# The experts' second product of a mixture-of-experts stage, from rounded pieces instead of full-precision matmuls

## What is computed

```python
buf = zeros((E * cap + 1, Dx)).at[safe].set(x_rep)          # E = 8, cap = 4560, Dx = 192
z = 2.0 * buf
z = z * rsqrt(mean(z * z, axis=-1) + EPS) * norm_w[:, None, :]
gu = einsum('ecd,ehd->ech', z, w13)                          # first product, 192 -> 1024
g, u = split(gu, 2, axis=-1)
y = buf + einsum('ech,edh->ecd', silu(g) * u, w2)            # second product, 512 -> 192
y_tok = y.reshape(E * cap, Dx)[didx]
out = (cw[:, None] * y_tok).reshape(N, TOP_K, Dx).sum(axis=1)
```

## Time and profile before

| | |
|---|---|
| median of 3 runs | 3388.71 us |
| lowest and highest | 3383.93 and 3389.58 us |
| span of the profiled execution | 3385.4 us |
| TensorE busy in the span | 3004.5 us |
| VectorE, GpSimd, ScalarE busy | 2468.5, 2034.5, 1363.1 us |
| mean granted TensorE clock | 0.944 of full speed |

### The profile page before, as it was taken

How to read it: one execution, slowest core, us unless ns; L and a number is a source line. 1 busy time by engine, 2 the same in 40 slices (tenths; PEclk the granted TensorE clock), 3 DMA queues, 4 the chain that set the end, 5 groups by cost and what they waited for, 6 DMA issues and landing times.

```text
span 3385.4 us, 62750 instructions
## 1 busy us (share of the span) xinstructions
PE 3004.5 (89%) x20432; PEld 2601.3 (77%) x20432; DVE 2468.5 (73%) x6258; ACT 1363.1 (40%) x3398; POOL 2034.5 (60%) x1558
## 2 busy tenths in 40 slices
PE   2988889888889888898898898599999999999997
PEld 1777767777777777777777777598989898898987
DVE  3899998999998999989989987354444444444553
ACT  0434444344344344343443444343344443443443
POOL 2666666666666666666666664255555555555655
PEclk9899998999998999989988989799999999999999
DMA  6544544433333333233233320233333333433333
GB/s 190 150 131 138 155 126 138 130 85 102 90 89 103 82 97 103 77 101 99 80 101 89 90 75 23 68 51 62 52 67 49 66 57 56 69 50 65 51 62 48
DMA packets 205961, 297.49 MB, mean 88 GB/s; under 512 B 88374, under 2 KB 167675, under 8 KB 205874
## 3 DMA queue, kind: packets, MB, share of 16 engines
q1 hardware_dynamic: 82994, 243.82, 26.1%
q0 software_dynamic: 122880, 52.55, 11.1%
HBM read 201.73 MB, written 93.90 MB: 87 GB/s over the span
## 4 chain that ended last, share of the span: by engine, by line
issue 31%; POOL 27%; DVE 20%; DMA 12%; PE 7%; POOLq 1%; SPq 1%; ACT 1%; DVEq 0%; ACTq 0%
DMA out<-arena,who 10%; POOL out L1437 8%; POOL moe_rows L1268 6%; POOL qk L721 4%; POOL arena L689 4%; DVE hot L631 3%; DVE place L669 3%; POOL rstd L707 3%; POOL spread L697 3%; DVE arena L1419 2%; DVE pooled L498 2%; DVE pieces L550 2%; PE bank L1409 2%; DVE rot_s L535 1%; DMA prob<-in_w_t 1%
## 5 line engine op out<-in xcount | busy, mean ns | idle before, releaser
L1437 POOL DMA_INDIRECT out<-arena,who x320 | 597.2, 1866 | 202.9 <-issue 198.7
L721 POOL TENSOR_TENSOR qk<-rot_c,rot_s 114x768 f32<-114x768 f32 x256 | 455.2, 1801 | 256.7 <-DVE rot_s L535 253.6
L1395 ACT ACTIVATE arena<-bank 128x456 f32<-128x456 f32 x320 | 175.5, 549 | 634.2 <-PE bank L1386 621.8
L1409 PE MATMUL bank<-prob,arena 128*114 128x192 f32 x2560 | 429.3, 326 | 0.0
L689 POOL TENSOR_TENSOR arena<-arena 112x896 f32<-112x896 f32 x192 | 396.8, 2096 | 44.3 <-DMA arena<-in_x 44.3
L1409 PEld LDWEIGHTS bank<-prob,arena 128*114 128x114 f32 x2560 | 412.2, 178 | 0.0
L1268 POOL DMA_INDIRECT moe_rows<-row,slot x256 | 293.1, 1145 | 185.3 <-issue 185.3
L1401 DVE TENSOR_TENSOR arena<-bank,arena 128x456 f32<-128x456 f32 x320 | 201.7, 630 | 268.5 <-ACT arena L1395 256.6
L571 DVE TENSOR_REDUCE top<-bank 114x2 f32<-114x456 f32 (+1 forms) x576 | 332.0, 622 | 2.5 <-PE bank L903 2.0
L843 PE MATMUL bank<-w_qkv,xn_t 97*114 97x384 f32 x512 | 221.3, 561 | 109.4 <-DVE place L669 108.7
L1426 POOL TENSOR_TENSOR rms<-rms,minus_half 114x4 f32<-114x4 f32 x82 | 85.4, 1042 | 348.0 <-DVE rms L1324 348.0
(11 more groups left out here) (167 smaller groups left out, 7523.2 us busy)
## 6 DMA issues: line engine op xcount, KB each, us to landing
arena<-in_x SPq DMA_DIRECT2D x64, 2352.0 KB, 11.3
arena<-moe_rows SPq DMA_DIRECT2D x82, 363.4 KB
moe_rows<-filler SPq DMA_DIRECT2D x20, 1453.5 KB
out<-h SPq DMA_DIRECT2D x64, 171.0 KB
out<-arena,who POOLq DMA_INDIRECT x320
arena<-in_w_t SPq DMA_DIRECT2D x9, 512.0 KB
arena<-in_w_t SPq DMA_DIRECT2D x18, 256.0 KB
moe_rows<-row,slot POOLq DMA_INDIRECT x256
```

The costliest lines, as they stand in the source:

```text
L721: nc.gpsimd.tensor_tensor(dst, a, b, ALU.add).then_inc(qk_rotated[t], 1)
L1409: ins = nc.tensor.matmul(bank[6 + s // 2][0:TT, D * (s % 2):D * (s % 2 + 1)], hid[:, j, TT * s:TT * (s + 1)], w_dn[e_par][:, j, :], start= ...
L1437: nc.gpsimd.indirect_dma_start(out=out[:, :], out_offset=bass.IndirectOffsetOnAxis(ap=who[par][:, s:s + 1], axis=0), in_=ys[par][:, s, :], ...
```

## The change

`hid` and `w_dn` are each split into a rounded part (fp32r) and the rest. `expert_down` multiplies the rounded part of `hid` by both parts of `w_dn` side by side (384 columns), and the rest of `hid` by the rounded part of `w_dn` (192 columns). Each of the four row groups gets a bank of its own: 6 and 7 as before, and 0 and 1, which `expert_up` uses for j = 0 and 2. The row groups are done in two pairs: pair 1 (banks 0 and 1) first, pair 0 (banks 6 and 7) behind it, partly interleaved. Each bank then holds two sums of 192 columns, and `weigh_rows` adds both, in eight operations in place of four, with a wait of VectorE for itself between the first part and the second. `expert_up` of the next tile waits for `y_first`, which pair 1 of `weigh_rows` sets. ScalarE gets four more copies for each tile (`high_hid`), VectorE four more subtractions (`low_hid`); both get one more operation for each expert. The order of the two engines' programs is changed around them.

```diff
         def round_expert(act, e, par):
...
+            nc.scalar.activation(w_dn2[par][:, :, 0, :], w_dn[par][:, :, :], ACT.Copy).then_inc(w_rounded, 1)
         def split_expert(dve, e, par):
...
+            nc.vector.tensor_tensor(w_dn2[par][:, :, 1, :], w_dn[par][:, :, :], w_dn2[par][:, :, 0, :].bitcast(fp32),
+                                    ALU.subtract).then_inc(w_split, 1)
         def expert_up(pe, n, e_par, j):
...
+            if j == 0:
+                wait(pe, y_first, n)
+        def high_hid(act, n, j):
+            act.wait_ge(hid_made, 4 * n + j + 1)
             if j == 0:
-                wait(dve, down, n)
+                wait(act, down, n)
+            nc.scalar.activation(hid2[:, j, 0, :], hid[:, j, :], ACT.Copy).then_inc(hid_high, 1)
+        def low_hid(dve, n, j):
+            dve.wait_ge(hid_high, 4 * n + j + 1)
+            nc.vector.tensor_tensor(hid2[:, j, 1, :], hid[:, j, :], hid2[:, j, 0, :].bitcast(fp32),
+                                    ALU.subtract).then_inc(hid_low, 1)
+        DOWN = (6, 7, 0, 1)
         def expert_down(pe, n, e_par):
-            wait(pe, y_weighted, n)
-            for j in range(4):
-                pe.wait_ge(hid_made[j], n + 1)
-                for s in range(SUB):
-                    ins = nc.tensor.matmul(bank[6 + s // 2][0:TT, D * (s % 2):D * (s % 2 + 1)], hid[:, j, TT * s:TT * (s + 1)],
-                                           w_dn[e_par][:, j, :], start=(j == 0 and s % 2 == 0), stop=(j == 3),
-                                           skip_group_check=True)
-            ins.then_inc(down, 1)
+            for pair, j in ((1, 0), (1, 1), (1, 2), (0, 0), (1, 3), (0, 1), (0, 2), (0, 3)):
+                if pair == 1:
+                    pe.wait_ge(hid_low, 4 * n + j + 1)
+                    if j == 0:
+                        pe.wait_ge(hid_made, 4 * n + 3)
+                elif j == 0:
+                    wait(pe, y_weighted, n)
+                for s in (2 * pair, 2 * pair + 1):
+                    at = slice(TT * s, TT * (s + 1))
+                    nc.tensor.matmul(bank[DOWN[s]][0:TT, 0:2 * D], hid2[:, j, 0, at],
+                                     w_dn2[e_par][:, j, :, :].rearrange("p c n -> p (c n)"),
+                                     start=(j == 0), stop=False)
+                    ins = nc.tensor.matmul(bank[DOWN[s]][0:TT, 0:D], hid2[:, j, 1, at], w_dn2[e_par][:, j, 0, :],
+                                           start=False, stop=(j == 3))
+                if j == 3:
+                    ins.then_inc(down_first if pair else down, 1)
+        def weigh_rows(dve, n, par, pair):
+            if pair:
+                dve.wait_ge(down_first, n + 1)
+                dve.wait_ge(x_weighted, n + 1)
+            else:
+                dve.wait_ge(down, n + 1)
+            for part in range(2):
+                for s in (2 * pair, 2 * pair + 1):
+                    ins = nc.vector.scalar_tensor_tensor(
+                        out=ys[par][:, s, :], in0=bank[DOWN[s]][0:TT, D * part:D * (part + 1)], scalar=w_slot[par][:, s:s + 1],
+                        in1=ys[par][:, s, :] if part else xw[:, s, :], op0=ALU.mult, op1=ALU.add)
+                if not part:
+                    ins.then_inc(y_begun, 1)
+                    dve.wait_ge(y_begun, 2 * n + 2 - pair)
+            ins.then_inc(y_first if pair else y_weighted, 1)
...
             def tile(n, e, e_par, par, pair, next_e):          # VectorE
                 make_hid(dve, n, 0)
                 make_z(dve, n1, par1)
+                make_hid(dve, n, 1)
+                low_hid(dve, n, 0)
+                make_hid(dve, n, 2)
+                low_hid(dve, n, 1)
+                low_hid(dve, n, 2)
+                make_hid(dve, n, 3)
+                split_za(dve, n1)
+                low_hid(dve, n, 3)
+                split_zb(dve, n1)
                 take_numbers(dve, n1, par1, pair1, next_e)
                 mean_square(dve, n + 2)
-                weigh_rows(dve, n, par)
+                weigh_rows(dve, n, par, 1)
+                weigh_rows(dve, n, par, 0)
...
             def tile(n, e, e_par, par, pair, next_e):          # ScalarE
                 silu(act, n, 0)
                 weigh_x(act, n, par)
+                silu(act, n, 1)
+                high_hid(act, n, 0)
+                silu(act, n, 2)
+                high_hid(act, n, 1)
+                high_hid(act, n, 2)
+                silu(act, n, 3)
+                round_za(act, n + 1)
+                high_hid(act, n, 3)
+                round_zb(act, n + 1)
                 square_rows(act, n + 2, par, pair + 1)
```

More of the change, by code:

```diff
@@ L170, in build @@
         w_qkv = sb("w_qkv", [C1, 2, 3 * D])
-        b_row = sb("b_row", [1, 3 * D])
-        b_fold = sb("b_fold", [1, 3 * D])
         w_out = sb("w_out", [C1, 2, D])
@@ L198, in build @@
         rot_s = sb("rot_s", [TT, 2, 2 * D])
+        b_row, b_fold = (r[0:1, :, :].rearrange("p t n -> p (t n)")[:, 0:3 * D] for r in (rot_c, rot_s))
         qk = sb("qk", [TT, 2, 2 * HEADS, 4, HD])
@@ L272, in build @@
         w_dn = [prob[:, 4 * D * i:4 * D * (i + 1)].rearrange("p (j n) -> p j n", j=4) for i in range(2)]
+        w_dn2 = [sb(f"w_dn2_{i}", [128, 4, 2, D], fp32r) for i in range(2)]
+        hid2 = sb("hid2", [128, 4, 2, ROWS], fp32r)
         sq = prob[0:TT, 8 * D:(8 + SUB) * D].rearrange("p (s n) -> p s n", s=SUB)
@@ L344, in build @@
         za_split, zb_split = sem("za_split"), sem("zb_split")
-        gate_up = [sem(f"gate_up{j}") for j in range(4)]
+        gate_up = sem("gate_up")
         silued = sem("silued")
-        hid_made = [sem(f"hid_made{j}") for j in range(4)]
+        hid_made = sem("hid_made")
+        hid_high = sem("hid_high")
+        hid_low = sem("hid_low")
         down = sem("down")
-        numbered, x_weighted, y_weighted = sem("numbered"), sem("x_weighted"), sem("y_weighted")
+        numbered, x_weighted, y_begun, y_first, y_weighted = (
+            sem(x) for x in ("numbered", "x_weighted", "y_begun", "y_first", "y_weighted"))
+        down_first = sem("down_first")
         added = [sem(f"added{i}") for i in range(2)]
@@ L362, in setup_sync @@
                 (w_qkv[0:C, :, :], w_attn.rearrange("(c p) n -> p c n", p=C)),
-                (b_row[:, :], b_attn.rearrange("(a n) -> a n", a=1)),
+                (b_row, b_attn.rearrange("(a n) -> a n", a=1)),
                 (rez[:, :], rezero.rearrange("(a n) -> a n", a=1).to_broadcast([C1, 1])),
@@ L395, in setup_sync @@
             sp.wait_ge(folded, 1)
-            sp.dma_start(w_qkv[C:C1, 1, :], b_fold[:, :]).then_inc(bias_placed, 16)
+            sp.dma_start(w_qkv[C:C1, 1, :], b_fold).then_inc(bias_placed, 16)
         x_img = x.rearrange("b (g c) (q r) w -> b (c q) g (r w)", g=NG, r=HALF)
@@ L1300, in split_expert @@
             for c in range(2):
-                ins = nc.vector.scalar_tensor_tensor(out=w_lo[par][:, c, :], in0=w_raw[:, c, :], scalar=nw[:, c:c + 1],
-                                                     in1=w_hi[par][:, c, :].bitcast(fp32), op0=ALU.mult, op1=ALU.subtract)
-            ins.then_inc(w_split, 1)
+                nc.vector.scalar_tensor_tensor(out=w_lo[par][:, c, :], in0=w_raw[:, c, :], scalar=nw[:, c:c + 1],
+                                               in1=w_hi[par][:, c, :].bitcast(fp32), op0=ALU.mult, op1=ALU.subtract)
+            nc.vector.tensor_tensor(w_dn2[par][:, :, 1, :], w_dn[par][:, :, :], w_dn2[par][:, :, 0, :].bitcast(fp32),
+                                    ALU.subtract).then_inc(w_split, 1)
         def square_rows(act, n, par, pair):
@@ L1352, in turn_z, with round_za, round_zb, split_za @@
             ins.then_inc(zb_turned, 1)
-        def round_z(act, n):
+        def round_za(act, n):
             act.wait_ge(za_turned, n + 1)
             nc.scalar.activation(za_hi[:, :], bank[4][:, 0:ROWS], ACT.Copy).then_inc(za_rounded, 1)
+        def round_zb(act, n):
             act.wait_ge(zb_turned, n + 1)
             nc.scalar.activation(zb_hi[:, :], bank[5][:, 0:ROWS], ACT.Copy).then_inc(zb_rounded, 1)
-        def split_z(dve, n):
+        def split_za(dve, n):
             dve.wait_ge(za_rounded, n + 1)
             nc.vector.tensor_tensor(za_lo[:, :], bank[4][:, 0:ROWS], za_hi[:, :].bitcast(fp32), ALU.subtract).then_inc(za_split, 1)
+        def split_zb(dve, n):
             dve.wait_ge(zb_rounded, n + 1)
@@ L1373, in expert_up @@
                 pe.wait_ge(zb_split, n + 1)
+            if j == 0:
+                wait(pe, y_first, n)
             if j >= 2:
-                pe.wait_ge(hid_made[j - 2], n + 1)
+                pe.wait_ge(hid_made, 4 * n + j - 1)
             else:
-                wait(pe, hid_made[j + 2], n)
+                wait(pe, hid_made, 4 * n + j - 1)
             hi, lo = w_hi[e_par], w_lo[e_par]
@@ L1386, in expert_up @@
                 ins = nc.tensor.matmul(dst, lo[:, 1, col], zb[:, :], start=False, stop=True)
-            ins.then_inc(gate_up[j], 1)
+            ins.then_inc(gate_up, 1)
```

(12 more changed lines are left out.)

11 lines of the change are left out of this document (2 added, 9 removed).

## The result

The changed kernel takes 3521.5 us (median of 4 runs) against 3389.1 us of the kernel before (4 runs): ratio 1.0394, 95% interval 1.038 to 1.0409. The kernel after is 3.9% slower. The forecast was 3522 us.

A forecast was written before the change was run, and what follows sets the result against it. The scatter loop (`weigh_rows`, scatter, landing, `take_numbers`) bounds the second stage. Per expert 8 x 1.57 + 2.6 = 15.2 us, times 8, plus 1.0 is 122; with 11 for clock, span 3385.4 gives 3518, median 3522; range 3490 to 3572.

The forecast's parts named there:

- What bounds the kernel: Second stage: the scatter loop at 14.57 us a tile sets the pace; TensorE's own loop, 14.2 us, has 0.3 slack.
- `weigh_rows`, 1.57 us: VectorE, inside the scatter loop: eight operations with two waits take 2.96 us in place of 1.39, 1.57 more a tile.
- the lower bound: For the added `weigh_rows` time: four more starts at 0.33 us and nothing for the waits, 1.3 us a tile.
- `expert_down`, 4.4 us: TensorE's second product: 4.4 us a tile, 0.7 less than before, giving nothing on the path that sets the end.
- the prediction's estimate by that rule: `expert_down` if weight loads did not overlap: 0.46 us a pair, 7.4 us; TensorE's work 16.5 us a tile, the bound.
- `high_hid` and `low_hid` at nothing: ScalarE copies, 2.2 us, and VectorE subtractions, 2.5 us a tile: cost nothing, the latter hidden by idle time before `take_numbers`.
- `y_first`, a gap of 2.6 us: TensorE before each next tile: its loop becomes 13.5 us, 2.6 below 16.1, so it idles 2.6 us a tile.
- The clock, 11 us: TensorE after gaps: 1.2 GHz stretches showing up to 0.8 us, in one tile of six, some 11 us in all.
- its rival: Lower TensorE clock comes back in almost every tile: 3545 to 3607 us, middle 3570; chance 0.18.
- The boundaries: Seven changes of expert weights: 2.6 us more in place of twice 1.57, since waits for weights hide part.
- the 13.5 of my walk: TensorE's new loop with `y_first`: 0.1, 8.35, 0.8, 2.7 of `expert_down` and 1.5 of weighing, 13.5 us a tile.
- the scatter loop: Closed loop of `weigh_rows`, GpSimd's scatters, landing, `take_numbers`, next `weigh_rows`: 14.57 us a tile before, 16.1 after.

The follow-up runs named there:

- the loop cut there: Kernel before with `take_numbers` moved behind `weigh_rows` in VectorE's order: 3393.0 us, ratio to before 1.0007.
- the kernel with the cut loop: Changed kernel with `take_numbers` moved behind `weigh_rows` in VectorE's order: 3406.6 us, ratio to before 1.0057.
- the run with the filled gap: Changed kernel with 11 more unread matmuls of 456 columns behind each tile's second product: 3520.2 us, ratio to before 1.039.
- the run with four weighings: Changed kernel with four weighing operations a tile in place of eight, second part left out of the output: 3417.9 us, ratio to before 1.0082.
- the best kernel: Changed kernel with `take_numbers` last, `mean_square` between the halves of `weigh_rows`, next weights issued before an expert's first two tiles: 3312.8 us, ratio to before 0.9779.

## Why the prediction was right, point by point

- **What bounds the kernel.** Right, and shown from both sides: lengthening `weigh_rows` alone in the kernel before costs 110 us, and cutting the loop in the changed kernel gives 115 back. But in the kernel before TensorE has less slack than 0.3 us a tile: the loop cut there gave nothing, as TensorE's own loop over a whole expert is as long (151.0 against 150.3 us).
- **`weigh_rows`, 1.57 us.** Measured 2.95 - 1.39 = 1.56 in the traces. The run that adds four operations without waits lengthened it by 1.30, the lower bound; the two waits are the other 0.26.
- **`expert_down`, 4.4 us.** Measured 4.4, and worth nothing there. (The line between the rows for 114 and 228 columns gives 0.099 us for 192, not the 0.096 of the sum; that is 0.05 us a tile.) The weight loads lie beside the matmuls as the rows said: a pair takes 0.28 us. The Trainium skill, "TensorE: Matmul & The Clock Gate", section "Part 3: Packing small matmuls", says that a weight load overlaps a matmul in flight only when their row groups differ; the prediction's estimate by that rule was 0.46 us a pair. The trace after disagrees with it, as the one before did.
- **`high_hid` and `low_hid` at nothing.** Right in the main: VectorE still waits for the landing in 58 of 66 tiles, 1.9 us before `take_numbers` in the tile shown.
- **`y_first`, a gap of 2.6 us.** Away from the boundaries the gaps are 2.2 to 2.8 us, or 0.5 to 1.1 behind a tile that ran partly at the lower clock. In the changed kernel that wait costs nothing in a steady tile; in the kernel with the cut loop it is what comes next.
- **The clock, 11 us.** This term was mis-sized: the run with the filled gap puts it at 1 us by the medians and at nothing in the steady tile. The lower clock came more often than in the one tile of six that I took (some 160 us of the stage ran at it, by the 0.94), but away from the boundaries the loss went into the slack. Two slips in its rival change nothing: 3511 + 40 x 0.8 is 3543, not 3545, and the middle of that case 3575, not 3570.
- **The boundaries.** The sum came out in spite of that because of two small terms that I had too low. The ten intervals of an expert together went from 150.3 to 166.9 us, 16.7 more before rounding, where I had 15.2. A steady tile grew by 1.65 and not 1.57 (0.1 in the scatter and its landing), and the four intervals at a boundary by 6.75 in place of 5.7. That leaves 1.5 us for each expert, 12 us in all, about what the clock did not take. So the mechanism was foreseen, but that the sum met the median within 1 us is luck: one term was some 10 us too high and the others some 12 too low.

What stays open: in the run with four weighings, the boundary costs some 1.7 us an expert more than before, and the pieces of `w_dn` are not the reason. The traces suggest `y_first`: before, TensorE worked ahead through j = 0 and 1 of the next tile while the weights were on their way, and its gaps were 4.3 us on average. In the run with four weighings it stands until `weigh_rows`, and they are 5.9 (6.4 in the changed kernel). No run isolates this. Nor is it shown why GpSimd's scatter lasts some 50 ns longer in the run with four weighings; more VectorE work beside it is no reason by itself, as the changed kernel has more and stays at 1873 ns. And the 13.84 us of the best kernel lie 0.3 above the 13.5 of my walk; what holds them is open.

## What to carry to other kernels

An engine that is 95% busy need not be the only bound: walk the waits round until they close, add the links up, and compare the sum with the tile's period. Work put behind a wait that closes such a loop costs its full length for each tile, however idle the engine is ahead of that wait; the same work ahead of it is free up to the idle time. In an in-order engine the cheapest repair can be to move a small step with a long wait (here two copies, 0.24 us together) behind the work that others wait for. When one loop is cut, measure the next bound: here three came close behind each other, at 14.6, 14.2 and 13.8 us a tile. Earlier weights at the boundaries gave 55 to 61 us, more than either of these steps (0.3 to 0.4 us in each of some 64 steady tiles). A size that fits the total can still hide two errors: compare term by term.

## What the runs showed of the hardware that I had not expected

- A TensorE gap of 2.35 us was followed by 3.2 us at 1.2 GHz, and in the attention stage one of 1.7 us by 10 us; yet filling the gaps left the time where it was (3520.2 against 3521.5 us): the gap of the next tile shrank by about the loss.
- GpSimd's scatter instruction took 1867 ns on average before, 1873 after, and 1916 in the run with four weighings; there the third of each four took 1.99 us in place of 1.85.
- On VectorE, eight operations with two waits for an own result took 2.95 us, and two plain groups of four 2.69: 0.13 us for each wait. That is small, but on the scatter loop it comes to 21 us in 80 tiles.
